# A deformable-convolution block and its experts on one core: VectorE reads every fourth bank of the remainders' transposed weights

## The reference

```python
x = x + conv(_ln_c(x), ...)            # x: (8, 16, 16, 64)
t = _to_tokens(x)                      # 2048 tokens of 64
x = t + ffn(_ln_t(t), ...)

# conv: deformable 3x3, 8 groups of 8 channels
x_proj = inputs @ w_in + b_in
x1 = gelu(layernorm(depthwise3x3(inputs) + dw_bias) * gamma + beta)
offset = x1 @ w_off + b_off            # two numbers per group and tap
mask = softmax(x1 @ w_mask + b_mask)   # over the 9 taps of a group
samp = bilinear_gather(pad(x_proj), base + tap + offset)
out = sum_over_taps(samp * mask) @ w_out + b_out

# ffn: 8 experts of 64 -> 256 -> 64, top 2 of a softmax router
h = gelu(xe @ W1[e] + b1[e]);  y = h @ W2[e] + b2[e]
out = sum over the two best experts of weight * y
```

## Time and profile before

| | |
|---|---|
| median of 3 runs | 329.78 us (328.94 to 332.53) |
| profiled execution | 327.07 us, span from first to last instruction 325.3 us |
| mean granted TensorE clock | 0.982 of full speed |
| busy: TensorE, its weight loads, VectorE, ScalarE, GpSimd | 284.0, 186.0, 243.7, 260.0, 107.5 us |
| units' reads by ScalarE | 144 high, 144 low, mean 602 ns each |
| first and last high read | 33.3 and 289.4 us |

### The profile page before, as it was taken

How to read it: one execution, slowest core, us unless ns; L and a number is a source line. 1 busy time by engine, 2 the same in 40 slices (tenths; PEclk the granted TensorE clock), 3 DMA queues, 4 the chain that set the end, 5 groups by cost and what they waited for, 6 DMA issues and landing times.

```text
span 325.3 us, 8588 instructions
## 1 busy us (share of the span) xinstructions
PE 284.0 (87%) x3369; PEld 186.0 (57%) x3369; DVE 243.7 (75%) x715; ACT 260.0 (80%) x484; POOL 107.5 (33%) x111
## 2 busy tenths in 40 slices
PE   8778798856899989989999799989979999987894
PEld 3543465633567765566667665665646556654462
DVE  5899968999958999896588988893656724456735
ACT  2663978879797899999978799999869988862863
POOL 5032323503442604063437050352533406164000
PEclk9799799999799999999999999999999999999998
DMA  7310000000000000000000000000000000000000
GB/s 156 99 32 0 2 4 3 1 2 0 2 3 2 4 2 0 2 2 8 3 11 2 2 2 2 1 11 0 10 2 2 2 1 2 10 0 11 0 2 17
DMA packets 5638, 3.39 MB, mean 10 GB/s; under 512 B 5073, under 2 KB 5278, under 8 KB 5534
## 3 DMA queue, kind: packets, MB, share of 16 engines
q1 hardware_dynamic: 5598, 2.84, 3.9%
HBM read 2.04 MB, written 0.52 MB: 8 GB/s over the span
## 4 chain that ended last, share of the span: by engine, by line
PE 37%; DVE 30%; ACT 20%; issue 9%; POOL 4%; POOLq 0%; DVEq 0%; ACTq 0%
ACT wk L1172 6%; PE m_ps L1468 6%; ACT wk L1167 5%; DVE prod L780 5%; PE zl_ps L1376 4%; PE zh_ps L1373 4%; PE m_ps L1451 3%; PE ga_ps L1391 3%; PE m_ps L1453 3%; PE ga_ps L1393 2%; PE ga_ps L1392 2%; ACT h_all L1194 2%; PE ga_ps L1434 2%; DVE w_low L818 2%; POOL y_r L482 2%
## 5 line engine op out<-in xcount | busy, mean ns | idle before, releaser
L1167 ACT ACTIVATE wk<-zh_ps 128x512 f16<-128x512 f32 x144 | 86.7, 602 | 25.6 <-PE zh_ps L1373 23.7
L780 DVE TENSOR_TENSOR prod<-ga_ps,wx 128x480 f32<-128x480 f32 x96 | 61.9, 652 | 42.3 <-PE ga_ps L1393 40.6
L1172 ACT ACTIVATE wk<-zl_ps 128x512 f16<-128x512 f32 x144 | 86.7, 602 | 0.1
L1391 PE MATMUL ga_ps<-v_all,wk 128*128 128x80 f16 x576 | 76.7, 203 | 7.6 <-DVE prod L780 6.7
L489 POOL TENSOR_TENSOR prod<-prod 128x960 f32<-128x960 f32 x16 | 35.6, 2228 | 138.7 <-DVE prod L780 138.7
L1392 PE MATMUL ga_ps<-v_all,wk 128*128 128x80 f16 x576 | 76.6, 203 | 0.0
L1393 PE MATMUL ga_ps<-v_all,wk 128*128 128x80 f16 x576 | 76.6, 203 | 0.0
L1391 PEld LDWEIGHTS ga_ps<-v_all,wk 128*128 128x128 f16 x576 | 57.1, 99 | 18.8 <-issue 8.2
L1392 PEld LDWEIGHTS ga_ps<-v_all,wk 128*128 128x128 f16 x576 | 57.7, 100 | 8.3 <-issue 0.5
L1373 PE MATMUL zh_ps<-tab,sel_hi 128*128 128x512 f16 x144 | 55.7, 387 | 6.5 <-ACT wk L1167 4.8
L1376 PE MATMUL zl_ps<-tab,sel_lo 128*128 128x512 f16 x144 | 56.2, 390 | 4.6
(11 more groups left out here) (269 smaller groups left out, 510.2 us busy)
## 6 DMA issues: line engine op xcount, KB each, us to landing
h_all<-in_W SPq DMA_DIRECT2D x1, 512.0 KB
w_s<-in_W SPq DMA_DIRECT2D x1, 512.0 KB
x_tok<-in_x SPq DMA_DIRECT2D x1, 384.0 KB, 4.1
out_dram<-x_tok SPq DMA_DIRECT2D x6, 64.0 KB, 2.2
w_high<-w_high SPq DMA_DIRECT2D x1, 256.0 KB, 2.8
const<-in_table SPq DMA_DIRECT2D x1, 218.0 KB, 3.0
vec<-in_vectors SPq DMA_DIRECT2D x1, 132.5 KB
x_tok<-in_x SPq DMA_DIRECT2D x1, 128.0 KB, 2.3
```

The costliest lines, as they stand in the source:

```text
L780: dve.tensor_tensor(prod[q % 2][:].rearrange("p k n -> p (k n)")[:, f * PB * NV:(f + 1) * PB * NV] .rearrange("p (n c l) -> p n c l", n=PB ...
L1167: act.activation(wk[n % WR][:, 0, :], zh_ps[:], ACT.Relu, scale=W_SCALE).then_inc(s_wkh, 1)
L1172: act.activation(wk[n % WR][:, 1, :], zl_ps[:], ACT.Relu, scale=W_SCALE).then_inc(s_wkl, 1)
L1391: pe.matmul(to, w_h, high, start=True, stop=False)
```

## The change

In units 3, 7, 11, ... 35 of every chunk (9 of 36, 36 in all) the bank `zl_ps` is read by VectorE in place of ScalarE, in one operation that takes the maximum with zero and multiplies by the scale. It counts its own semaphore `s_wkv`. TensorE's waits for a low read become `wait_low(at)`: if the read numbered `at` is one of VectorE's, it waits for `s_wkv`, otherwise for `s_wkl` with VectorE's reads subtracted. ScalarE's low read of such a unit is left out, with its wait. VectorE's new step has places of its own, one unit ahead: unit 3 at 2, unit 7 at 6, and so on (unit 15 at 15 in the middle chunks). Many other places in all tables change by half a unit to a few units. Those of steps that the text speaks of are in the cut below. Counts and sizes of all other work stay.

```diff
+LOW_UNITS = range(3, NP, 4)
...
+        vector_fills = [units_done(j, n) for j in range(CHUNKS) for n in LOW_UNITS]
+        def moved_by_vector(at):
+            return sum(fill < at for fill in vector_fills)
...
+            def weights_low(j, n):
+                dve.wait_ge(s_zl, units_done(j, n) + 1)
+                if NP * j + n >= WR:
+                    dve.wait_ge(s_ga, fills_done(NP * j + n - WR + 1))
+                dve.tensor_scalar(wk[n % WR][:, 1, :], zl_ps[:], 0.0, W_SCALE, ALU.max, ALU.mult).then_inc(s_wkv, 1)
...
+                    for i, u in enumerate(LOW_UNITS):
+                        if n == at["weights_low"][i]:
+                            weights_low(j, u)
                     for m in range(FILLS):
                         if (PB * m + PB - 1) // TP == n:
                             weigh(j, m)
...
-                        weights_low(j, int(n))
+                        if int(n) not in LOW_UNITS:
+                            weights_low(j, int(n))
...
+            def wait_low(at):
+                by_vector = moved_by_vector(at)
+                if by_vector and moved_by_vector(at - 1) < by_vector:
+                    pe.wait_ge(s_wkv, by_vector)
+                else:
+                    pe.wait_ge(s_wkl, at - by_vector)
...
-                pe.wait_ge(s_wkl, units_done(j, n))
+                wait_low(units_done(j, n))
```

Places (of the tables for VectorE, chunk 0 and middle chunks; `rows` and `lane_sum` are lists of steps):

```diff
-DVE_FIRST: "input_stats": 26.5, "input_norm": 32, "input_low": 0.5, "conv_stats": 9, "conv_norm": 13, "rows": [18, 18, 18, 21]
+DVE_FIRST: "weights_low": [2, 6, 10, 14, 18, 22, 26, 30, 34], "input_stats": 23, "input_norm": 31.5, "input_low": 1.5,
+           "conv_stats": 10, "conv_norm": 11.5, "rows": [17, 18, 20, 23]
-DVE_MIDDLE: "input_stats": 17, "project_low": 5.5, "edges": 20.5, "tap_weights": [24.5, 31.5], "expert_weights": 23.5
+DVE_MIDDLE: "weights_low": [2, 6, 10, 15, 18, 22, 26, 30, 34], "input_stats": 20.5, "project_low": 7, "edges": 22,
+            "tap_weights": [24.5, 27], "expert_weights": 23
-ACT_FIRST: "pad_image": 2.5, "image_out": 9.5     ACT_MIDDLE: "hidden": [..., 23.5, 24.5, 25.5, 26.5, 28.5, 29.5, 30.5, 31.5]
+ACT_FIRST: "pad_image": 0.5, "image_out": 10.5    ACT_MIDDLE: "hidden": [..., 22.5, 23.5, 24.5, 25.5, 27.5, 28.5, 29.5, 30.5]
```

More of the change, by code:

```diff
@@ L60 @@
[L60 to L69, removed]
+            "offsets": 15.5, "table": [26.5, 29.5], "samples_t": 12, "project_out": 5, "experts_t": 10.5, "router": 9,
@@ new lines @@
+            "expert_in": [6, 12.5, 12.5, 14.5, 15.5, 21, 25, 27, 31.5, 34.5, 34.5, 35.5, 35.5, 35.5, 35.5, 35.5],
+            "expert_out": [11.5, 14, 15, 18.5, 20.5, 23, 25.5, 26], "outputs_t": [28.5, 35.5], "b2": 25}
+ACT_FIRST = {"pad_image": 0.5, "project_high": 6.5, "image_out": 10.5, "conv_gelu": 14.5, "tap_exp": 21.5, "hat_x": 25.5,
+             "samples_out": 3, "zn_out": 18.5, "router_exp": 3.5,
+             "hidden": [2, 16, 18, 18, 18.5, 23, 28, 29, 35.5, 35.5, 35.5, 35.5, 35.5, 35.5, 35.5, 35.5],
+             "outputs_out": [31, 27.5]}
@@ new lines @@
+DVE_FIRST = {"weights_low": [2, 6, 10, 14, 18, 22, 26, 30, 34], "input_stats": 23, "input_norm": 31.5, "input_low": 1.5,
+             "conv_stats": 10, "project_low": 6.5, "conv_norm": 11.5, "image_out": 11, "positions": [15.5, 16],
+             "rows": [17, 18, 20, 23], "edges": 22.5, "columns": 21, "tap_weights": [24.5, 28],
+             "lane_sum": [10, 10, 19, 19, 28.5, 28.5, 1, 2], "residual": 0.5, "inner_norm": 7, "zn_low": 1,
+             "route": [9, 14.5, 14.5], "expert_weights": 19, "b2": 25.5, "bias_rows": 4, "router_parts": 0,
+             "w1_low": [10, 14.5, 19.5, 24.5], "outputs_in": [26, 10.5]}
@@ new lines @@
+POOL_FIRST = {"tap_tree": [6, 10, 27, 35], "combine": [31.5, 23], "conv_rstd": 7.5, "inner_rstd": 15, "input_rstd": 29.5}
+PE_MIDDLE = {"input_t": 0, "convolve": [4, 6.5, 7.5, 7.5], "project": 6.5, "image_t": [9.5, 11.5], "conv_t": 12.5,
+             "offsets": 15.5, "table": [30.5, 35.5], "samples_t": 3.5, "project_out": 4, "experts_t": 8.5, "router": 12,
+             "expert_in": [11, 12.5, 13.5, 15, 16.5, 18.5, 19.5, 21, 22, 23, 24.5, 25, 27, 28, 29, 29],
+             "expert_out": [17.5, 19, 20.5, 23, 27, 28, 30.5, 32.5], "outputs_t": [25.5, 35.5], "b2": 34.5}
@@ L70 @@
 ACT_MIDDLE = {"pad_image": 2.5, "project_high": 6.5, "image_out": 10.5, "conv_gelu": 14.5, "tap_exp": 17.5, "hat_x": 27.5,
-              "samples_out": 3.5, "zn_out": 9.5, "router_exp": 17.5,
-              "hidden": [12.5, 12.5, 14.5, 15.5, 18.5, 19.5, 19.5, 21.5, 23.5, 24.5, 25.5, 26.5, 28.5, 29.5, 30.5, 31.5],
+              "samples_out": 3.5, "zn_out": 9.5, "router_exp": 18.5,
+              "hidden": [12.5, 12.5, 14.5, 15.5, 18.5, 19.5, 19.5, 21.5, 22.5, 23.5, 24.5, 25.5, 27.5, 28.5, 29.5, 30.5],
@@ L73 @@
               "outputs_out": [23.5, 32.5]}
[L74 to L84, removed]
@@ L85 @@
-ACT_LAST = {"pad_image": 7, "project_high": 11.5, "image_out": 12.5, "conv_gelu": 16.5, "tap_exp": 15, "hat_x": 13.5,
+DVE_MIDDLE = {"weights_low": [2, 6, 10, 15, 18, 22, 26, 30, 34], "input_stats": 20.5, "input_norm": 28.5, "input_low": 3,
+              "conv_stats": 8, "project_low": 7, "conv_norm": 9, "image_out": 10.5, "positions": [16, 16],
+              "rows": [18, 18, 18.5, 19], "edges": 22, "columns": 23, "tap_weights": [24.5, 27],
+              "lane_sum": [9.5, 13.5, 19.5, 21.5, 28, 28, 0.5, 1], "residual": 4, "inner_norm": 4.5, "zn_low": 9,
+              "route": [12, 12.5, 12.5], "expert_weights": 23, "b2": 14, "bias_rows": 4, "router_parts": 0,
+              "w1_low": [7, 8.5, 13.5, 14.5], "outputs_in": [24, 34.5]}
@@ new lines @@
+POOL_MIDDLE = {"tap_tree": [14.5, 18, 26.5, 35.5], "combine": [34.5, 35.5], "conv_rstd": 16.5, "inner_rstd": 1.5,
+               "input_rstd": 28.5}
+PE_LAST = {"input_t": 10.5, "convolve": [3.5, 6.5, 11.5, 12.5], "project": 3.5, "image_t": [8, 18.5], "conv_t": 14.5,
+           "offsets": 11.5, "table": [28, 19], "samples_t": 4.5, "project_out": 5, "experts_t": 9, "router": 12,
+           "expert_in": [12, 13, 14, 15.5, 18.5, 18.5, 19.5, 20.5, 22.5, 23.5, 24, 25.5, 27.5, 28, 30, 30],
+           "expert_out": [17.5, 18.5, 20.5, 23, 26.5, 27, 31.5, 32], "outputs_t": [24, 33.5], "b2": 23.5}
```

23 lines of the change are left out of this document (10 added, 13 removed).

## The result

The changed kernel's median is 340.53 us (4 runs, 336.95 to 343.45) against 331.15 for the kernel before (4 runs): a ratio of 1.035, 95% interval 1.027 to 1.044. The forecast was 329.6, no change, with a range to 335.5. It is slower, and outside the range.

The account below looks back on a forecast made before the run. No engine alone was the bound: VectorE bound chunk 0's full stretch, ScalarE was fullest or nearly so late in middle chunks. Chunk 0 +2.7, chunks 1 and 2 -2.0, chunk 3 -0.9: -0.2 us, so 329.6 us, range 324.0 to 335.5.

Parts of the forecast that it names:

- The relief of ScalarE: ScalarE loses 36 evictions, 0.48 us each; counted -2.4 us per middle chunk, -1.5 in chunk 3, 1.0 in chunk 0.
- it does nothing: Rival: the single bank's 1.08 us round trip decides, whoever reads; 329.8 us; chance 0.42 together with the forecast.
- It stands a little later in any case, so I count VectorE's time and not this stall.: Chunk 0, unit 19, near 65 us: TensorE stands 2 us or so for VectorE; that stall was left unpriced.
- unit 27: Middle chunks: VectorE's eviction 1.1 us late, covered by ScalarE's two long activations; +0.1 us, or 1.1 without that cover.
- The work on VectorE: 36 evictions of 0.69 us, pitch 0.60: +2.4 us in chunk 0's full stretch, +1.2 per middle chunk, +0.6 in chunk 3.
- Chunk 3: VectorE has room, 33 of 61 us busy; relief of 1.5 us against +0.6 in the early part: -0.9 us.
- The places: Steps shifted by half a unit to five units inside one chunk; counted at nothing.
- The new deadline: VectorE's deadline shrinks from 1.5 units to one, 1.9 us, less the 1.08 us trip: 0.8 us.
- One sign of being wrong: The prediction is wrong if waits on VectorE's new group add up to more than ScalarE's relief.
- The faster one: Rival: ScalarE's relief counts in full and VectorE's load falls into its waits; -5.3 us, 324.5 us; chance 0.30.
- The moved column weights: Rival, middle chunks: they block products by up to 1.6 us until ScalarE's activation is done; 334.8 us; chance 0.08.
- The slower one: Rival: VectorE becomes the bound in three chunks, through evictions later than the bank is wanted; +7.1 us, 336.9 us; chance 0.20.

Follow-up runs that it names:

- relief_alone: Kernel before with ScalarE's nine reads per chunk left out in chunks 1 to 3 and done by nobody; 329.57 us, ratio 1.001 (0.996 to 1.007).
- wait_only: Kernel before, ScalarE keeping all reads, with VectorE waiting as for nine reads per chunk, a one-column operation, and TensorE waiting for it; 340.02 us, ratio 1.037.
- load_only_2: Kernel before with 36 unused 128x512 operations added on VectorE, TensorE waiting for none, ScalarE keeping all reads; 337.87 us, ratio 1.024.
- late_half: Changed kernel with only 15 reads moved, 14 of them 1.1 us or more late there; ScalarE keeps the other 21; 341.78 us, ratio 1.035.
- places_only: Changed kernel's places, but ScalarE keeps all reads of the remainders' bank; 333.56 us, ratio to the kernel before 1.011 (1.003 to 1.018).
- picked: Kernel before, its own places, with only the 8 reads moved for which VectorE stood idle, none in chunk 0; 329.04 us, ratio 1.001.

## Why the prediction was wrong

**The relief of ScalarE** (forecast -2.4 us in each middle chunk, -1.5 in chunk 3). This is the first wrong term. I took a busy share of 95% for a bound and priced a read at its whole pitch of 0.48 us. With 1.0 us in chunk 0 the sum held 7.3 us of relief. relief_alone measures 0.06 us a read, 2.2 us for 36. ScalarE's work arrived at TensorE's pace: with fewer reads its waits for the next bank grew, 23.7 us to 39.7 in the changed kernel. What sets that pace isn't shown. The round trip of the low bank, the rival "it does nothing", isn't enough for it, since relief_alone took this trip out of nine units of a chunk and gained no more than that.

**"It stands a little later in any case, so I count VectorE's time and not this stall."** This is the second, and the larger one: the sum held 0.2 us for late reads in each middle chunk and nothing in chunk 3, and wait_only shows the wait alone at 2.3, 3.2 and 2.6 us there. TensorE standing early isn't the same as standing later: in the stall of chunk 3 ScalarE worked only 0.83 of 4 us, so it ran dry too. Of unit 27 I had the lateness wrong, 2.3 and 3.0 us in the changed kernel where I had 1.1. The cover held in part: the next low matmul fell a further 0.4 and 1.0 us behind the kernel before.

**The work on VectorE.** 684 ns per read against 0.69 forecast. For chunk 0 load_only_2 gives +2.9 (in a body that scatters by 1.3) against +2.4 for its full stretch: no contradiction. For the middle chunks +2.2, and +2.6 with a fall of the clock, against +1.2: the forecast had half. For chunk 3 +0.2 against +0.6.

**Chunk 3.** I weighed engines by their share and found room. Unit 7 is late by 3 us there not because VectorE is full but because its queue stands on GpSimd. The trace of before showed that wait in chunk 3, and I didn't lay the reads' places against it.

**The places.** Counted at nothing, they cost 1.1% without the move (1.003 to 1.018), with +0.8 and +0.4 us in the middle bodies at full clock, and with the move they save an estimated 2.5 us in each middle chunk (4 less the 1.5 of a fall of the clock).

**The new deadline.** The prediction named it rightly, 0.8 us of slack where the products have 1.5 units. The reads that missed it by far carry the loss (late_half 1.035). The step that failed is that I didn't turn it into a price. One sign of being wrong was named: waits on the new group above ScalarE's relief. They are 12.6 us on TensorE against the 2.2 above.

**The rivals.** The faster one, relief in full and VectorE's load in its waits, falls with relief_alone. The moved column weights blocked nothing: in the changed kernel's trace they waited for ScalarE only once, in chunk 0's first (39.2 us). The slower one, 336.9 us, names the deciding point, an eviction that starts later than its bank is wanted, and gives +7.1 us against 9.4 measured in the medians. Its mechanism is half right: it has VectorE as the bound and nothing lost in chunk 3, but the chain has less VectorE than before, and chunk 3 lost 2.9. It had a chance of 0.20.

**What stays open.** Chunk 0 grew by 8.2 us in the changed kernel's trace, 2.1 more than with the move alone, and neither half of the reads shows it. Part of it is that execution's clock. places_only and late_half run the same instructions up to unit 10 of chunk 0; from its first read to the low matmul of unit 10 (places_only, then late_half):

```profile
37.50:56.80 19.30, 16.24 (x231) 11.15 (x232) 10.00 (x21) 14.49 (x25) 3.95 (x3) 0.82 0.02 2
```

```profile
37.50:55.10 17.60, 14.16 (x231) 9.52 (x231) 9.73 (x21) 14.44 (x25) 3.95 (x3) 1.00 0.02 3
```

19.3 us at a clock of 0.82, 17.6 at full clock. The changed kernel took 19.4 us there, at 0.82, so some 1.7 us of its 8.2 are no work of the moved reads. Its fastest timed execution, 336.95 us with a span of 335.1 at a mean clock of 0.980, leaves chunk 0 an estimated 64.4 us, if head (33.3), the other bodies (202.6) and tail (34.8) took what the traces show, and up to 66 if chunk 3 was spared its fall of the clock. How the rest of the 8.2 us splits between places, reads and clock, these traces don't settle. The head's 2 us more in the changed kernel's profile lie in its own scatter.

## What to carry to other kernels

Before a read of a single-buffered bank is given to another engine, lay the moment at which the bank is full against that engine's queue, instance by instance, and price each lateness as time of the producer; the receiver's busy share doesn't tell it. One late read of 0.7 us cost 2 us, a fall of the clock included, on an engine with half its time free; in wait_only's middle chunks a lateness of up to 1.1 us cost next to nothing. A queue that is 95% busy is not a bound until work taken away from it moves the end: the cheapest test is to leave the work out. When steps of a hand-written order are moved, look at what will run beside them: here four small operations took 3.41 us in place of 0.98 beside GpSimd's.

## What the runs showed of the hardware

Four VectorE operations of 128x64 with two constants per partition took 0.98 us with GpSimd idle and 3.41 us beside its additions of 128x960 and 128x320. The read of PSUM kept 671 to 692 ns in all 36 instances of the changed kernel, beside GpSimd's work or not.

After the same stretch of work TensorE's clock sometimes falls and sometimes doesn't. picked and before are equal to 0.02 us from the start of chunk 2 to its unit 12. Two stretches of picked, then the same two of before, counted from the start of the chunk:

```profile
180.70:184.70 4.00, 2.54 (x56) 2.08 (x54) 3.96 (x10) 3.04 (x6) 0.00 (x0) 1.00 0.02 4
184.70:188.10 3.40, 3.27 (x21) 2.49 (x22) 3.16 (x17) 1.57 (x3) 0.00 (x0) 0.50 0.00 0
```

```profile
179.92:183.92 4.00, 2.53 (x56) 2.06 (x54) 3.96 (x10) 3.02 (x6) 0.00 (x0) 1.00 0.01 4
183.92:187.32 3.40, 3.29 (x43) 2.71 (x44) 3.16 (x17) 2.25 (x5) 0.00 (x0) 1.00 0.00 0
```

In the first stretch TensorE does the same, 2.54 and 2.53 us busy with 56 matmuls. In the second its clock is 0.50 (1.2 GHz) in picked and full in before, and it gets through 21 matmuls in one and 43 in the other. picked was 1.56 us behind after it, and still 1.38 at unit 35.

The head goes by steps of 2 us, and its clock with it: 33.3 us at a clock of 0.95, 35.4 at 0.86, 37.4 at 0.82. I take such falls for the larger part of this kernel's scatter of 1%; that isn't tested.
